# Weighted one-hots of a product-key FFN: one instruction for each of the three weight parts in place of one for all three

## What is computed

```python
q = (x_norm @ wq).reshape(B, T, HEADS, 2, DIM_KEY)
sim = jnp.einsum('bthpd,hkpd->pbthk', q, keys)
s1, i1 = jax.lax.top_k(sim[0], K)           # 16 best of 64, for each of 8 heads
s2, i2 = jax.lax.top_k(sim[1], K)
...
final_scores, pk = jax.lax.top_k(all_scores, K)
final_idx = jnp.take_along_axis(all_idx, pk, axis=-1)
...
hidden = jnp.einsum('btd,bthkd->bthk', x_norm, wd)
hidden = jax.nn.gelu(hidden, approximate=False)
hidden = hidden * jax.nn.relu(final_scores)
out = jnp.einsum('bthk,bthkd->btd', hidden, wu)
```

## Time and profile before

| | |
|---|---|
| median of 3 runs | 1328.29 us (1323.45 to 1329.32) |
| the profiled execution | 1320.42 us; from its first to its last instruction 1318.6 us |
| busy in that span | PE 1079.4, DVE 1085.9, POOL 517.9, ACT 395.0 us |
| mean granted TensorE clock | 0.903 of full |
| weighing on POOL, L746 | x118, 330.9 us |
| DVE L1186, L1183, L1199 | x128 each: 159.3, 76.8, 131.2 us |

### The profile page before, as it was taken

One profiled execution on the slowest core, in us unless ns is written; L12 is line 12 of the kernel. 1 busy time (PEld: TensorE's weight loads), 2 busy tenths in 40 slices (PEclk: granted clock), 3 DMA queues, 4 the chain that ended last, 5 costly groups with the idle time before them and its releaser, 6 DMA issues.

```text
span 1318.6 us, 28688 instructions
## 1 busy us (share of the span) xinstructions
PE 1079.4 (82%) x10152; PEld 743.2 (56%) x10152; DVE 1085.9 (82%) x5027; ACT 395.0 (30%) x724; POOL 517.9 (39%) x467
## 2 busy tenths in 40 slices
PE   4799987796877762467897997989887989899998
PEld 2344433242223221356776876877776878778887
DVE  2667556979999998699999999999999999995621
ACT  1256554443434540121221222222221222222211
POOL 5230410502012012235646556565646564655500
PEclk9799998998778885658998999999998989999999
DMA  4344313222111101700000000010000010000000
GB/s 155 100 147 134 119 58 113 69 70 76 48 45 39 50 10 36 305 2 1 24 6 27 24 10 24 2 32 15 24 11 24 2 32 15 24 10 27 2 17 9
DMA packets 59925, 63.76 MB, mean 48 GB/s; under 512 B 6882, under 2 KB 56164, under 8 KB 59268
## 3 DMA queue, kind: packets, MB, share of 16 engines
q1 hardware_dynamic: 59780, 61.90, 14.4%
HBM read 42.21 MB, written 19.66 MB: 47 GB/s over the span
## 4 chain that ended last, share of the span: by engine, by line
DVE 47%; PE 36%; issue 6%; POOL 5%; DMA 3%; ACT 2%; SPq 2%; DVEq 0%; POOLq 0%; ACTq 0%; another core or an unknown queue 0%
PE bank L1229 34%; DVE mem L1186 6%; DVE mem L1152 4%; DVE mem L1199 4%; DVE mem L1018 3%; DVE mem L1019 3%; DVE mem L1183 2%; DVE mem L1087 2%; PE bank L1232 2%; DVE mem L1023 2%; DVE mem L1015 2%; DVE mem L1027 2%; DVE mem L1039 2%; DVE mem L1083 1%; DVE mem L1090 1%
## 5 line engine op out<-in xcount | busy, mean ns | idle before, releaser
L1229 PE MATMUL bank<-mem 128*128 128x32 bf16 (+5 forms) x9672 | 1030.7, 278 | 158.3 <-issue 66.6
L1229 PEld LDWEIGHTS bank<-mem 128*128 128x128 bf16 (+3 forms) x9672 | 691.0, 125 | 449.1 <-issue 211.9
L746 POOL TENSOR_TENSOR mem<-mem 128x1536 bf16<-128x1536 bf16 x118 | 330.9, 2805 | 291.2 <-DVE mem L1186 250.2
L1152 DVE TENSOR_REDUCE mem<-bank 128x1 f32<-128x512 f32 x256 | 167.5, 681 | 81.3 <-PE bank L1229 81.0
L845 ACT ACTIVATE mem<-bank 128x512 f32<-128x512 f32 x256 | 148.7, 601 | 209.6 <-PE bank L1229 208.8
L1199 DVE TENSOR_TENSOR mem<-mem 128x512 f32<-128x512 f32 x128 | 131.2, 1025 | 81.2 <-ACT mem L882 76.8
L882 ACT ACTIVATE mem<-bank 128x512 f32<-128x512 f32 x128 | 76.6, 598 | 342.4 <-PE bank L1229 342.4
L1186 DVE TENSOR_TENSOR mem<-mem 128x2048 bf16<-128x2048 bf16 x128 | 159.3, 1244 | 0.0
L1232 PE MATMUL bank<-mem 128*128 128x128 f32 (+3 forms) x480 | 75.4, 288 | 77.6 <-POOL mem L669 26.5
L891 ACT COPY mem<-bank 128x512 f32<-128x512 f32 x128 | 74.9, 586 | 167.2 <-PE bank L1229 167.2
L1232 PEld LDWEIGHTS bank<-mem 128*128 128x128 f32 (+3 forms) x480 | 54.9, 141 | 122.7 <-issue 95.3
(11 more groups left out here) (99 smaller groups left out, 749.8 us busy)
## 6 DMA issues: line engine op xcount, KB each, us to landing
mem<-parts_d SPq DMA_DIRECT2D x192, 64.0 KB, 2.3
parts_d<-mem SPq DMA_DIRECT2D x16, 384.0 KB, 2.6
mem<-in_L_ffn_expert_down SPq DMA_DIRECT2D x16, 256.0 KB, 2.9
downT_d<-mem SPq DMA_DIRECT2D x16, 256.0 KB, 3.1
mem<-downT_d SPq DMA_DIRECT2D x4, 1024.0 KB, 9.5
mem<-in_L_ffn_expert_up SPq DMA_DIRECT2D x4, 1024.0 KB, 17.3
tok_d<-mem SPq DMA_DIRECT2D x16, 160.0 KB, 1.8
mem<-tok_d SPq DMA_DIRECT2D x16, 160.0 KB, 2.4
```

The source lines that it names most:

```text
L746: nc.gpsimd.tensor_tensor(ow[q % 2], i0, i1, ALU.mult).then_inc(ow_rdy, 1)
L1152: nc.vector.tensor_reduce(nmx[g % 2][:, i % TB, i // TB:i // TB + 1], psum[n % 3][:, :], AX.X, ALU.max, negate=True).then_inc(s_max, 1)
L1229: return nc.tensor.matmul(o, l, r, start=first, stop=last)
```

## The change

The three parts of the weight are multiplied one after the other by three instructions of 512 elements, on POOL and on DVE in the fill. Each of the three adds 1 to the semaphore, so everyone who waits for weighed blocks waits for three times the number: PE and DVE still wait for a block as a whole. `WP` is 3.

```diff
             if isinstance(c, int) and c in OWN:
-                eng.wait_ge(ow_own, OWN.index(c) + 1)
+                eng.wait_ge(ow_own, WP * (OWN.index(c) + 1))
             elif isinstance(c, int) and c < 16:
                 if c >= 0:
-                    eng.wait_ge(ow_rdy, c + 1 - sum(o < c for o in OWN))
+                    eng.wait_ge(ow_rdy, WP * (c + 1 - sum(o < c for o in OWN)))
             else:
-                eng.wait_ge(ow_rdy, c + (1 - len(OWN)))
+                eng.wait_ge(ow_rdy, c * WP + WP * (1 - len(OWN)))
...
-        def weighing(q, tt):
-
-            i0 = oj[q % 2].unsqueeze(1).to_broadcast([P, 3, TP, JL, PAIR])
-            w = tt[:, q % BPT, 2:5, :].rearrange("p w (a t) -> p w a t", a=TP)
-            return i0, w.unsqueeze(3).to_broadcast([P, 3, TP, JL, PAIR])
+        WP = 3
+
+        def weighing(q, tt, w):
+
+            part_of = tt[:, q % BPT, 2 + w, :].rearrange("p (a t) -> p a t", a=TP)
+            return oj[q % 2], part_of.unsqueeze(2).to_broadcast([P, TP, JL, PAIR])
...
-                i0, i1 = weighing(q, tokT[2 * (1 - par) + q // BPT])
-                nc.gpsimd.tensor_tensor(ow[q % 2], i0, i1, ALU.mult).then_inc(ow_rdy, 1)
+                for w in range(WP):
+                    i0, i1 = weighing(q, tokT[2 * (1 - par) + q // BPT], w)
+                    nc.gpsimd.tensor_tensor(ow[q % 2][:, w], i0, i1, ALU.mult).then_inc(ow_rdy, 1)
...
-                    i0, i1 = weighing(q, tt)
-                    nc.vector.tensor_tensor(ow[q % 2], i0, i1, ALU.mult).then_inc(ow_own, 1)
+                    for w in range(WP):
+                        i0, i1 = weighing(q, tt, w)
+                        nc.vector.tensor_tensor(ow[q % 2][:, w], i0, i1, ALU.mult).then_inc(ow_own, 1)
```

## The result

The changed kernel takes 1341.85 us as a median of four runs (1339.25 to 1348.57); the kernel before took 1325.94 in four runs beside it (1323.45 to 1329.32). The ratio is 1.0117, with a 95% interval of 1.0082 to 1.0153: slower by 16 us, and by more than the 0.5% that can be told from no change. The forecast was 1339 us, range 1325 to 1356. The profiled execution took 1344.19 us, with a span of 1342.4 and a mean granted clock of TensorE of 0.890; before it was 1320.42, 1318.6 and 0.903.

The account below looks back on a forecast made before the run. DVE was taken to bound the middle stretch (98% busy), PE the end. Terms 8.8-1.7+2.1+1.7 = +10.9 us on the profiled 1320.42 gave 1331.3; with 7.9 carried over to the median, 1339 us, range 1325 to 1356.

Parts of the forecast that it names:

- The price of a piece: POOL: a 512-element piece takes 1.045 us, so a block of three takes 3.055 us, 0.295 us longer.
- the cover of 0.47 us: Slots with searches: L746 ends 0.47 us before L1199 starts, which hides the 0.295 us, so nobody waits.
- Rivals B: No change: queued pieces of 0.98 to 1.02 us hide more of the fixed part, 1328 to 1333 us; chance 0.2.
- C: Slower by far: pieces of 1.151 us, about +36 us, 1364 us; chance 0.1.
- The turns alternate: POOL and DVE both queued: the engine that did not hold goes next; each turn saves 0.14 or 0.13 us.
- Rival A: Faster: the long DVE waits are cut and stay cut, -36 us in the middle stretch, 1292 us; chance 0.12.
- rival D: POOL keeps its turn through its three pieces: all 55 lose 0.295 us, +18 to +20 in all, 1347 us; chance 0.08.
- The keys: DVE's L1066 waits 2.44 us and looks like a gain, but L1068 follows and takes the next turn: no gain.
- The sum of DVE's waits in the middle: Middle stretch, 55 DVE instructions behind POOL: +8.8 us, and -1.7 us for two L1183 in the first third.
- The late blocks: Middle stretch, three times POOL is late: L1199 gets a turn inside the block, which ends 0.7 us later: +2.1 us.
- The fill: 534 to 589 us: +1.1 us for DVE's own 10 blocks, +0.6 for POOL blocks L1183 waits for: +1.7.
- The end: From 1172 us on PE sets the time, DVE has 35 us over and POOL 43: 0.

## Why the prediction was right, point by point

**The price of a piece: right.** 1.044 us against 1.045. The block without disturbance:

```profile
655.59 3.04 POOL L748 TENSOR_TENSOR mem<-mem 128x512 bf16<-128x512 bf16 x3 [2.41 <-DVE mem L1188]
...
658.82 0.67 DVE L1202 TENSOR_TENSOR mem<-mem 128x512 f32<-128x512 f32 x1
```

3.04 against 3.055. It is also the search slot: the block ends at 658.63 and L1202 starts at 658.82, so the cover of 0.47 us has shrunk to 0.19 and still holds. Rivals B (pieces of 0.98 to 1.02) and C (1.151) fall with these rows.

**The turns alternate: right.** Rival A falls with the same sum of 4.38 us at 780.98, rival D (POOL keeps its turn) with the block of 3.67 us there, which DVE stretched. In the second third, at 646.92 us after and 632.40 before, DVE needs 3.13 us from L1202's start to L1188's end against 2.99: +0.14, forecast +0.15. In the last third, at 621.42 and 607.21, it is 2.79 against 2.51: +0.28, forecast +0.295. These are the places that the prediction was worked out from, or ones like them. What the turns cost over all places is the next step but one.

**The keys: right.** L1066 fell as the earlier trace rows could suggest, and the sum did not. Timeline after:

```profile
679.37 3.56 POOL L748 TENSOR_TENSOR mem<-mem 128x512 bf16<-128x512 bf16 x3 [2.10 <-DVE mem L1188]
679.61 1.09 DVE L1068 TENSOR_SCALAR mem<-mem 128x400 int32<-128x400 int32 x1
...
680.62 1.41 DVE L1070 SCALAR_TENSOR_TENSOR mem<-mem 128x400 int32<-128x400 int32 x1
...
681.95 1.41 DVE L1074 TENSOR_TENSOR mem<-mem 128x400 int32<-128x400 int32 x1
```

From 679.61 to 683.36 it is 3.75 us, before from 664.50 to 668.28 it was 3.78.

**The sum of DVE's waits in the middle: too high, and no growth is shown.** The term was 8.8 - 1.7 = +7.1 us. There are three executions on either side, since in the middle stretch the kernel with pieces on DVE alone does what the kernel before does, and the kernel with pieces on POOL alone what the changed one does. Each stretch is cut at its marks:

```
                           middle stretch   DVE busy   DVE idle   PE idle
before                          587.1         574.4      12.7      66.0
before, a second time           589.6         572.5      17.1      67.1
pieces on DVE alone             589.2         575.5      13.7      69.6
after                           594.4         577.0      17.4      74.3
after, a second time            594.0         575.3      18.7      69.8
pieces on POOL alone            598.0         571.3      26.7      74.8
```

DVE runs the same instructions in all six, and its busy time holds its waits for turns. It grew by 0.4 us between the means, with 3 to 6 us between executions of the same code. The stretch grew by 6.8 us, and 6.4 of them are DVE's idle time. A count by place agrees. If one adds up, beside each weighed block, by how much a DVE instruction exceeds the shortest of its line (where that is over 0.1 us), the sums are 71.2, 69.6 and 73.0 us before and 74.2, 73.2 and 69.3 after. By the third of 2.76 us in which the first such instruction comes, a block lost 2.3 us before and 2.2 after in the first third, 1.20 and 1.29 in the second, 0.40 and 0.64 in the last, with 15, 27 and 11 blocks in the three before and 14, 26 and 11 after. So the mis-sized step is the price that the prediction gave each event from three clean places: +0.15 in the second third is +0.09 as a mean, +0.295 in the last is +0.24, and 11 blocks stood there, where it had counted 16 instructions. Where only one or two DVE instructions meet the block, its last piece runs beside the searches, and the first third gained a little.

**The late blocks: right in kind, too low.** The term was +2.1 us. Timeline after, where the earlier trace rows had a wait of 1.04 us for PE:

```profile
724.44 6.68 POOL L748 TENSOR_TENSOR mem<-mem 128x512 bf16<-128x512 bf16 x6
...
725.33 0.71 DVE L1202 TENSOR_TENSOR mem<-mem 128x512 f32<-128x512 f32 x1
...
729.51 0.59 ACT L893 COPY mem<-bank 128x512 f32<-128x512 f32 x1 [6.81 <-PE bank L1232]
729.51 0.70 DVE L1185 TENSOR_TENSOR mem<-mem 128x512 bf16<-128x512 bf16 x1 [3.48 <-PE bank L1232]
```

L1202 slipped in for 0.71 us instead of 2.43, and DVE waited 3.48 us for PE instead: the 1.72 us that it saved were waited out again, and 0.7 more. That is the forecast 0.7 at L1185's start. L1185 itself then waits less, and by L1188's end 0.4 us are left, here (6.87 us from L1202's start against 6.46) and at the two other places (5.27 against 4.86 and 4.85): 1.2 us for the three, forecast 2.1. The same places vary by 2 us without the change: in the second execution of before this one took 8.19 us, with a wait of 4.20 for PE.

What the term left out is larger. DVE's idle time grew by 6.4 us between the means of the table above. Ahead of L1185 it waits for PE for 7.0 us in place of 4.4, and ahead of L1202, mostly for ACT, for 12.2 in place of 8.3. The cause as far as the traces tell it is the longer block in all the other slots: PE starts its product when the block is weighed, ACT's gelu comes later, and DVE waits for it. The place in the end, below, shows the first step of this to a tenth of a us; the rest of the chain is read from the waits. The two terms together were forecast at +9.2, and the middle stretch grew by 6.8 us between the means. That the sum comes so near is in part luck: the waits for turns gave 0.4 us of the 7.1 forecast, and the late blocks 6.4 in place of 2.1.

**The fill: not resolved.** Forecast +1.7; 51.8 and 53.9 us before, 54.0 and 54.1 after, and 52.6 with pieces on POOL alone. The single price fits. After:

```profile
574.57 0.79 DVE L1185 TENSOR_TENSOR mem<-mem 128x512 bf16<-128x512 bf16 x1
575.28 2.06 DVE L1188 TENSOR_TENSOR mem<-mem 128x2048 bf16<-128x2048 bf16 x1
...
577.26 1.08 DVE L1195 TENSOR_TENSOR mem<-mem 128x512 bf16<-128x512 bf16 x3
```

DVE's own three pieces take 1.08 us against 0.945, +0.14 for a forecast 0.11, and the pair ahead of them, from 574.57 to 577.34, 2.77 us against 2.64 from 560.69.

**The end: forecast 0, measured +1.5** (145.4 and 145.5 us before, 146.9 twice after). PE sets it, as said, at 83.3 of 88 us. The 1.45 us come at one place, 5 us into the stretch. Before:

```profile
1175.31 3.20 POOL L746 TENSOR_TENSOR mem<-mem 128x1536 bf16<-128x1536 bf16 x1
...
1178.61 1.66 PE L1229 MATMUL bank<-mem 128*128 128x32 bf16 x49 [2.20 <-issue]
```

After:

```profile
1197.61 6.10 POOL L748 TENSOR_TENSOR mem<-mem 128x512 bf16<-128x512 bf16 x4
...
1202.36 0.80 PE L1232 MATMUL bank<-mem 128*128 128x32 bf16 x26 [3.46 <-DVE mem L1188]
```

L746 ended at 1178.51, and PE started its product 0.10 us later. After, the block is the first three of the four pieces in the row. The third ended at 1202.26, and PE started 0.10 us later again. (The profile names L1188, but that had ended at 1201.36.) L1199, L1202 after, held POOL's first instruction up alike in both. Between the pieces L1185 and L1188 now got their turns too, so the block took 4.65 us where it had taken 3.20: 1.45 us, the whole growth of the end. Behind this place PE has the same waits of over 0.3 us in both kernels, 1.45 us later (1.23, 1.23 and 0.74 us). The pair with the input in the bank shows the same, 143.1 us and 144.5 with three pieces. So the sum lacks a fourth late block, and it priced a late block at 0.7 us for one short turn of DVE inside it, where here two fall into it, one of them the 1.2 us of L1188.

**The sum.** Forecast +10.9 for what the change does, measured +8.5 between the means of the second phase (6.1 to 10.8 by pairs) and +11.5 with POOL's pieces alone. The medians are 16 us apart, and the 5 us and more beyond the forecast are what stays open above: they lie in none of the prediction's steps. The forecast of 1339 us lies 3 us under the measured 1341.85 partly because it started from 1328.29, and before took 1325.94 beside the changed kernel.

## What to carry to other kernels

When two engines take turns on something that each instruction holds to its end, cutting the long instruction shortens each wait and not their sum, as long as the other engine has its next instructions of the same kind right behind. Look first at what follows the waiting instruction: with work behind it that needs no turn the pieces gained 7 us in the stretch, with such instructions behind it they lost about 6. Then look at who waits for the long instruction's result: with the other engine's turns inside it the result comes later (3.20 us became 4.65), and here nearly all of the loss was idle time behind that, not waits for turns. The surer step is to take one of the two out of the turns, here by leaving an operand in its bank, which gave 19 us between the medians.

## What the runs showed of the hardware

- A product of VectorE with one operand in a bank takes no turn with GpSimd: 128 of them took 0.662 to 0.692 us, and 42 of these started while a weighing of 2.76 us ran. With both operands in SBUF 47 of 128 started so, and the longest took 2.921 us.
- GpSimd's two-input instruction on bf16 has a fixed part that halves of a piece show too: 0.351 us at 88 elements, 0.612 at 256, 1.044 at 512, 2.76 at 1536. The steps between them are 1.55, 1.69 and 1.68 ns an element, and 0.18 to 0.21 us is left at zero.
- The two engines take turns, so a block of POOL in pieces grows by DVE's turns: 3.04 us undisturbed, 3.67 with DVE in between at 780.60, 4.65 at 1197.61, where DVE also had the turn ahead of it.
- The same first phase, with the same instructions, took 533 to 549 us from run to run. Two executions of the same kernel part behind a wait for a DMA of 4.51 or 0.96 us, with a granted clock of 0.65 or 0.99 in the same 35 us. A single profile of this kernel can't show a change under 1% by its span. Cutting it at marks can, down to the 4.5 us by which the second phase of the same kernel scatters.
